# The sum over the experts moved from VectorE to GpSimd, with new instruction orders

## The reference

```python
        out = jnp.zeros_like(x_flat)
        for e in range(N_EXPERTS):
            h = jax.nn.gelu(x_flat @ w1[e] + b1[e], approximate=False)
            y = h @ w2[e] + b2[e]
            out = out + comb[:, e:e + 1] * y
```

## Time and profile before

| | us |
|---|---|
| median of 3 runs (lowest to highest) | 3891.53 (3889.09 to 3901.82) |
| the profiled execution: its own time | 3896.18 |
| its span, first to last instruction | 3893.9 |
| DVE busy | 3420.1 |
| PE busy | 3127.3 |
| ACT busy | 2925.3 |
| POOL busy | 1337.2 |

### The profile page before, as it was taken

How to read it: one execution, slowest core, us unless ns; L and a number is a source line. 1 busy time by engine, 2 the same in 40 slices (tenths; PEclk the granted TensorE clock), 3 DMA queues, 4 the chain that set the end, 5 groups by cost and what they waited for, 6 DMA issues and landing times.

```text
span 3893.9 us, 31221 instructions
## 1 busy us (share of the span) xinstructions
PE 3127.3 (80%) x8728; PEld 1368.3 (35%) x8728; DVE 3420.1 (88%) x4654; ACT 2925.3 (75%) x3806; POOL 1337.2 (34%) x644
## 2 busy tenths in 40 slices
PE   5655878889787788979888888979788887877797
PEld 3231423334343333424343333424343333432232
DVE  1499979999898999999999999999999998999822
ACT  2546887987868888787888878787888879686442
POOL 0254333333323334343433443343433433333200
PEclk8757788989888899989999999989989999888797
DMA  1233333424324243333434342343424333333310
GB/s 63 77 108 96 113 109 92 128 80 135 99 94 118 93 131 95 119 118 109 125 98 123 107 131 94 121 117 109 124 95 126 104 116 104 104 119 104 100 49 11
DMA packets 209022, 404.60 MB, mean 104 GB/s; under 512 B 25936, under 2 KB 34256, under 8 KB 208592
## 3 DMA queue, kind: packets, MB, share of 16 engines
q1 hardware_dynamic: 206800, 398.41, 32.8%
q0 software_dynamic: 2048, 4.20, 1.0%
HBM read 387.57 MB, written 14.94 MB: 103 GB/s over the span
## 4 chain that ended last, share of the span: by engine, by line
PE 37%; DVE 26%; ACT 25%; issue 12%; POOL 0%; DMA 0%; DVEq 0%; ACTq 0%; POOLq 0%
PE bank_a L569 8%; DVE states L921 7%; PE bank_b L580 7%; ACT L705 6%; DVE states L927 6%; ACT decay L705 6%; DVE y_sum L932 3%; ACT L701 3%; ACT tok L705 3%; ACT last L705 3%; ACT middle L705 3%; PE bank_p L478 1%; PE bank_c L397 1%; PE bank_p L421 1%; PE bank_c L640 1%
## 5 line engine op out<-in xcount | busy, mean ns | idle before, releaser
L1199 POOL TENSOR_TENSOR dbu<-dtu,b_rows 128x1024 f32<-128x1024 f32 x512 | 1243.4, 2431 | 2104.1 <-DVE states L921 1823.6
L921 DVE TENSOR_TENSOR_SCAN states<-decay,dbu 128x512 f32<-128x512 f32 x1024 | 1298.7, 1311 | 38.1 <-ACT decay L705 30.5
L705 ACT ACTIVATE decay<-dt,neg_a 128x508 f32<-128x508 f32 x1024 | 659.4, 707 | 64.6 <-DVE states L921 59.0
L705 ACT ACT_TABLE_LOAD x516 | 662.0, 1283 | 47.5 <-PEq L344 16.6
L569 PE MATMUL bank_a<-middle,experts 128*128 128x512 f32 x1024 | 616.2, 687 | 97.1 <-ACT middle L705 88.9
L705 ACT ACTIVATE middle<-bank_a,columns 128x512 f32<-128x512 f32 x608 | 417.8, 687 | 329.6 <-PE bank_a L569 305.4
L927 DVE TENSOR_TENSOR states<-states,c_rows 128x512 f32<-128x512 f32 x960 | 610.8, 679 | 0.3
L932 DVE TENSOR_TENSOR y_sum<-y_sum,states 128x512 f32<-128x512 f32 x960 | 609.9, 674 | 0.2
L580 PE MATMUL bank_b<-middle,experts 128*128 128x512 f32 x1024 | 572.7, 643 | 21.4 <-ACT middle L705 11.8
L705 ACT ACTIVATE last<-bank_c 128x512 f32<-128x512 f32 (+2 forms) x320 | 201.0, 634 | 198.0 <-PE bank_c L617 52.4
L701 ACT ACT_TABLE_LOAD x232 | 297.7, 1283 | 46.0 <-PE bank_p L469 17.0
(11 more groups left out here) (206 smaller groups left out, 3944.7 us busy)
## 6 DMA issues: line engine op xcount, KB each, us to landing
b_rows<-bc_scratch SPq DMA_DIRECT2D x512, 256.0 KB, 3.4
c_rows<-bc_scratch SPq DMA_DIRECT2D x512, 256.0 KB, 3.3
experts<-ew SPq DMA_DIRECT2D x128, 512.0 KB, 3.5
comb_rows<-comb_scratch SPq DMA_DIRECT2D x128, 256.0 KB, 3.8
h_scratch<-tok SPq DMA_DIRECT2D x16, 256.0 KB, 3.3
x_scratch<-xin SPq DMA_DIRECT2D x16, 256.0 KB, 3.8
xr<-x_scratch SPq DMA_DIRECT2D x16, 256.0 KB, 4.9
h<-h_scratch SPq DMA_DIRECT2D x16, 256.0 KB, 5.3
```

Of the source, the lines that this page charges most:

```text
L705: return nc.scalar.activation(out, in_, func, **more)
L921: tick(nc.vector.tensor_tensor_scan(hs[:, h, ::step], da[:, n % DECAYS, h, ::step], dbu[:, n % AHEAD, h, ::step], 0.0, ALU.mult, ALU.add), ...
L1199: tick(nc.gpsimd.tensor_tensor(dbu[:, n % AHEAD], dtu[:, k % 2], row, ALU.mult), "a_dbu")
```

## The change

DVE's e_t writes even experts into x1 and odd ones into part. The add is a `gpsimd.tensor_tensor` on POOL, in a stream C of its own there. e_t of expert e waits for the add of e - 2 (from e = 2), the first norm of the next group, which writes x1, for the add of expert 6, and the router, which writes part, for that of expert 7. All five ORDER strings are replaced: DVE's is 128 letters shorter, POOL's 129 longer, the others have their old length. Matmuls, activations and transfers are the same in number and size, apart from the table loads that follow from ACT's order.

```diff
@@ ORDER
     "POOL": (
-        "APPPPPPAAAAAAAAAAAAAAAAAAAAAAAAAAPAAPAAAAAAAAAAAAAAAAAAAAAAAAAAAAAAAAAAPAAPAAAAAAAAAAAAAAAAAAAAAAAAAA"
...
+        "ACPPPPPPAAAAAAAAAAAAAAAAAAAAAAAAAPAPAAAAAAAAAAAAAAAAAAAAAAAAAAAAAPAACPAACAAAACAAAAACAACAAACAAACAAACAAAA"
+        "AAAAAPACPAAACAAACAAAACCCCAAACAAAAAAAAAAAAAPACPAACAAACAAAACAAACAAACACCAAAAAAAAAAAAAAPACAACPAACAACAAAAA"
...
@@ -1050,7 +1049,11 @@
             def middle(g):
                 q = 3 * g
-                yield from ln("c_", q, A, s_sq, x1)
+                yield
+                if g:
+                    dve.wait_ge(s["e_acc"], NE * g - 1)
+                dve.wait_ge(s["c_rs"], q + 1)
+                tick(tt(x1, A, s_sq, ALU.mult), "c_ln")
                 yield from ln("c_", q + 1, B, s_sq, x1, "mc1")
...
                 yield
+                if g:
+                    dve.wait_ge(s["e_acc"], NE * g)
                 dve.wait_ge(s["e_lg"], g + 1)
...
                     dve.wait_ge(s[f"e_cb{n % 2}"], 16 * (n // 2 + 1))
-                    if n:
-                        dve.wait_ge(s["e_acc"], n)
+                    if e > 1:
+                        dve.wait_ge(s["e_acc"], n - 1)
                     dve.wait_ge(s["e_y"], NF * (n + 1))
-                    tick(stt(part, B, col(f"eb2_{e}"), cb[:, e % 2], ALU.add, ALU.mult), "e_t")
-                    yield
-                    if e == 0 and g >= 2:
-                        dve.wait_ge(s["a_out"], g - 1)
-                    if e == 0:
-                        dve.wait_ge(s["c_h1"], g + 1)
-                    dve.wait_ge(s["e_t"], n + 1)
-                    tick(tt(h2[g % 2], h2[g % 2] if e else h1[:, :], part, ALU.add), "e_acc")
+                    tick(stt((x1, part)[e % 2], B, col(f"eb2_{e}"), cb[:, e % 2], ALU.add, ALU.mult), "e_t")
@@ the gpsimd block
+            def middle(g):
+                for e in range(NE):
+                    n = NE * g + e
+                    yield
+                    if e == 0 and g >= 2:
+                        pool.wait_ge(s["a_out"], g - 1)
+                    if e == 0:
+                        pool.wait_ge(s["c_h1"], g + 1)
+                    else:
+                        pool.wait_ge(s["e_acc"], n)
+                    pool.wait_ge(s["e_t"], n + 1)
+                    tick(nc.gpsimd.tensor_tensor(h2[g % 2], h2[g % 2] if e else h1[:, :], (x1, part)[e % 2], ALU.add), "e_acc")
...
-            drive("POOL", A=each(scan), P=each(gather))
+            drive("POOL", A=each(scan), P=each(gather), C=each(middle))
```

More of the change, by code:

```diff
@@ new lines @@
+        "PCCDPDCCDCCDCCDPCCPCCPPPDCCPPCCDCCPCCPCPCCCPPCCPCCPCCCCCCPDDCCPPPCCCCPCCPPPCCCPCCCPPPCCCPCCPPCDDCPPC"
+        "CCCPCCDDCPDPCDDCDDCDDPDCDPPCDPPCCDPPCCCPDCPCPCCDDPDDCCDPCCPCCDPCCDDPCCDPPDCCPPDCCPPDCCPDDPCCCCDCCPCC"
+        "DCCPPDDPDDCCDCCCCCDCCCDCCDCCDCCDDPCCDCCDCCPPDCCPCCCCPCDCCPPCDPCPDDCCPPPPCCDCCPPDPCPCPDDPDCPCDDDPCDDP"
+        "PCPPDDCCPPCCCDPCCPCPCCDCPDDCCDCCDCCDCCDDPPCCDPCCDDPPCCPPDCCDPCCPPDCCDCCPDPDCCPCCDCCDCCPCCPCCPDDDDDCC"
+        "CCDCDCCCDCCDCCDDPCCDCCDCCDPPCCPCPDPPCDDPDCPDCCPPDPCPCCPPCDDCPCDPCPDCPDDPCDDCPCPPCPPCCCDPPCCPDDCPCCDC"
@@ new lines @@
+        "DDDPDCCCCDCCDDPPCCPCCPDCCDDCCDCCDCCPCCDPPPCCPPDCCDDCCCCPDCCDCPCCCPCCDDDPDDPPPCCDDDCCDDCCDDCCPDCCPPDC"
+        "CPPCCPPDDPCCDDPCPCCPCPPDDPPCPCCPCCPCCPCPDDCDPCPPCPPDDDCDCDPPDDCPCCPDCCPCCDDDPDPCCDCDCCCDDPCCPDCCDDPC"
+        "CDPDPCCPDPPCCDCCPCDCCCDPPDCCDPCCPPCCPDDDDDCCCCCCDCDCCCDCCDCCDPPPCCDDCCPPCCDCCPPDCCPCCCCPCDCCPPCDPPCD"
+        "DCCPPPCPCDPCCDCPCCPDDCDPCDPPDPPCPPDDDCCPCDCPCCPCCCDDPDPCCDCCDCCDCCDCDCCCDDPPCCDPCCDDPPCCPPPDCCDPCCDD"
+        "PDCCPCDCPPDPPCCDCCDDDDCCDCCPCCPPDDDPCCDCCDDPCCDCCDCCDPPPCCCPCCCPPDDPPCCPPCDCCPDCPDPDCPPCCPDDCCPPDCCP"
@@ new lines @@
+        "PCCDDCDPPCPDDPCDDPCDCCCDCCDCCDCCDCDCCCDCCDDPPCCDCCDCCDCCDCCPCCDPDCCPDCCPPCCPPPDCCPDCCPDDPDCCPCCDCPPC"
+        "CCPDDDCCDDCCDCDCCCDDCCDPCCDCCDPPCCPPCCPPDDPCDCCPDCPPCPPDCCPPDPCPCPCCPCPDDCPCDPPCDDCDDCPPDDDCPPCPCDPC"
+        "CPCCDPDDCCCDPDCCCDCCDDPPCCDPCCPDPPCCPPDCCPDCCDPPDCCDCCDCCPCCDCPPCDPDCCDDDDCCDCCPCCPPCCDDCCDCCDCDCDPC"
+        "CDPCCDCCPPDCCPCCCCPCDCCPPCDPPCDPPDPCPCCCPCCPCPDCDPCCCPPPPCDDPPCCDPCPCCDDDPDCCDDDPDCCDCCDCCDCCDCCDCCP"
+        "DDDPCCDPCCDDPPCCDDPCCPPDPCCPDCCPDDPCCPCCDCCDCCPCCPCPCDDDDDCCPCCPPCCDDPDCCDCCDDPCCDCCDCCPPDCCPPPPCCPP"
@@ new lines @@
+        "DPCPDCCPCDPDCPDPCPCCCDPCCPPCDDPPCPPDCDDPCDPDDCDDPCDCCCDCCDCCDCCDCDCCCDCCDDPPPCCDPCCPPDCCPPDCCPPCCDDD"
+        "CCPDCCPCCPCCDDPDPPCCPDDDCCDDDCCPCCPPPPDCCPDCCDCCDCCPDDCCDCCDCCPDPCCPCCCCPCCDPPDPCPDCCPCDPCPDPCPCCCDP"
+        "CCPPCDDPPCPPDCDCDPDDPDCPDDCDCCCCCDCCDCCDCCDCCDCCDCCDDPPCCCCDCCDCCDCDCCCPCCDPDCCDCCPCCPPPDCCPPDCCDCCP"
+        "CCDCCPCCPCCDDDDPDCCPCCPCCPDDCCDCCDDCCPDDCCCPDPCDPPCPPCCDPDCCPDCCDPPPPCDPPCDPCPCPDDDCPCPCCDPCCCDPPCCD"
+        "PPCCDPPCCDPDCCPDDDPCCDDPCCDCDCCCDCCDDPPCCPDCCPPDCCPPDCCDPPCCDPCCPDDCCPCCDDPDPPCCPDDCCDDDDPCCPPDCCDCC"
@@ new lines @@
+        "DCDCCCDDCCDPPCCDCCDPCCCCPCDPCDPPPPPPCPDCDPCPCCPDPCPCCCDPCPPCPPDDDCCDDPPDDDCDPCDCPCPCCCDPDPCCDCCDCCDC"
+        "CDCCDCCDDPPCCDDPCCDDPPCCPPPDCCPDCCDPDPDCCPCCCCDCCDCCPCCPCCPDDDDDCCDDDCCDCCDDPCCDCCDCCPPDCCPPPCCCCPCC"
+        "DPDPPCCPDCDPPCCPPCDDPCPCCPCCPCPCCDDCPDCDDCPPDDDCDCPPDDPPPCCCDPCCPCCDDDDCCCDDDCCCCCCCCDDCCCDCCDCCCCCC"
+        "DCCDDCCDCDCCCCCCCDCCCCDCCDDDDCCDCCCCCCDCCDCDCDDCCDDCCDCDCCDCDDDCDCCDCCCCCDDCDCDCDDCCCCCCCDCCDCCDCDCC"
+        "CDDCCDCCDCCDCCDCCDCCDDCCCCDCCDCCDCDCCCCCDCCCDCDCCDCCDCCDCCCCDCCCCDCDCCCDDDCCCDDCDDDDDDDDDDDDCDCDDCDC"
@@ L73 @@
+        "CDCCDCCDDCDCDDDCDDCDCDCDCCCDCCDCCDCCDCCDCCDCCDCCCCDCCDCCDCCDCCCCCCCCCCCCCCCCCCCCCCCCCCCCCCCCCCCCCCCD"
         "DDDDDDDDDDDDDDDDDDDDDDDDDDDDDDDDDDDD",
@@ new lines @@
+        "PDCPCDPCCPCDCPPDAADACDDACPCPACDPCDPCPDCPDCPAAAADPADPCCCCPPCAAPDPDPCDPDCCCCCCDCDCDCDCPDCDPCCCPAAAACAP"
+        "CDDCPAAPCDCPDAADAAPCCPCDAPDCACPDDPDPCACDPCCPCCPCPADAACDCDCDCDDAAAPCPCDPCDPCPCDPCPDCAAAAPDCDAPACPPCCC"
+        "PCPAADDADAPDPACCCCCDCDCDCDCADPCDPAAAACPDPCADDCPDAADAPCCPACPCDACDAPCDCPADPDCCPCPCPCPCDCAADAADPADPCDCC"
+        "DDAACPCPACPDCDCCDCPCDPCAAAADCDACPCPCCPCPDADDAAAPDAPPCPAPCPDACDDCDCPDCDPCPAAAAPCDDCPAAACPDCADPADPCCPC"
+        "CPCPCDAADAPCPCDAADPCDACDPCCPCPADAADCDPCDCDDACPACPDCDPCDPCDPCCPCDAADAAAPCPACPPCPPAPDDADPDACCCCCCDCAAA"
@@ new lines @@
+        "DAPAAADACAAAAACADADDPDDDADAAADAADAADDDADCAAAADAAAAADAPADAAAACDDAADAAAACAAAAADADAPDPAAAAAAACAAAAAAAAA"
+        "ADDDDCAPAAAAAAACAAAAAAACAPDADADPAPDAAPAAACDAACADACDACADCCCCCDAAAPAAAAAADAPAAAAACAADADDADDDADAACADADA"
+        "ACDDDADAAAAADACAAADAADAAAACDDAAADAAAAAAAACDADAADACAAAAAAAAAACAAADADADDACAAAAAAADADADADAAAACDAAACAACA"
+        "CACCCCCAAAADAADAACDAAAADAAAAACADAAAAACAADADDADDDADAADAACDAADDDADCAAAADAAAAACDAADADDAAAADAACAAAAAADAA"
+        "DAACDAAAAAADAAADAADAADAAADDCDDDDDDDDDDCDDDCCDCCCCCCDDDDDCDDCDCCCCCCDDDDDDDDDDDDDDDDDDDDDDDDDDDD",
@@ L167 @@
+        "AAAAACAAAAACAAAAAAACCCAACADDCAAAAAAAAAAADAAAAAAAAAAAAAACAACAACAAAAAACAAAACAAACAAACAAAAAACCCAAAAAACAA"
+        "AAACADACCCCDCCCCD",
         "",
```

159 lines of the change are left out of this document (60 added, 99 removed).

## The result

The changed kernel takes 3944.74 us (median of 4 runs, 3932.79 to 3949.21) where the kernel before took 3890.31 us beside it (3888.19 to 3901.82): ratio 1.0127, 95% interval 1.0101 to 1.0153. The forecast was 3864, its range ended at 3926; rival D had 3944. One execution of all, of 10096 us in the kernel with the old head, is left out of its ratio. The profiled execution took 3946.3 us with a span of 3944.5, 50.6 more than before.

What follows compares the result with a forecast made beforehand. DVE was taken to bound the 3526 us between head and tail. Terms -81 + 60 - 25 + 6 + 11 + 1 = -28 gave 3868 us profiled, 3864 as run median; range 3812 to 3926 (8 in 10).

Steps and rivals of the forecast that it cites:

- rival D: Slower by order: groups 5 to 12 idle 18 us instead of 6.6, 91 in place of 11; 3944 us, chance 0.10.
- what the adds do to DVE: Scans and POOL's adds exclude each other in SBUF; scans that meet adds lose 60 us in all (bounds 0 and 122).
- -81: DVE's full stretch: removing the adds saves 72 us of queue and 9 us from adds that met POOL.
- +60: DVE's full stretch: time lost waiting for POOL's adds, 60 us by the count of windows.
- in the 3526 us between, DVE is the bound: From DVE's first scan to behind its last: DVE sets the time, busy 211.5 of 218.1 us in group 8.
- the middle groups: Groups 5 to 12: new strings no longer repeat, 8 groups x 1.4 = 11 us more (bounds 0 and 91).
- groups 1, 3 and 14: Fewer ACT table loads there, 71 us less ACT; of DVE's 77 us idle, 25 us go (bounds 0 and 77).
- Head and tail: Head: more ACT work before the first decay, +6 us (bounds 0 and 12); tail: last add before PE's norm, +1.
- the fourth term: The sum's term for groups 5 to 12, whose new strings don't repeat: +11 us.
- They also drain other streams: Argument against taking the idle of groups 13 and 14, with irregular strings, as the measure for groups 5 to 12.

## Why the prediction was wrong

**Right: what the adds do to DVE.** -81 and +60 make -21. DVE's stretch from first to last scan less its idle went from 3334.6 to 3314.1 us (3526.0 less 191.4, 3556.0 less 241.9): -20.5. DVE's busy time is 3394.0 (forecast 3385), table loads 700 (700), POOL's add 1274 ns in the median (1280), as these rows show, the second for the adds of the earlier trace rows. The scans' mean is 1335 ns, where 1355 was forecast: in the changed kernel the scans took 24 us more than before, and the rest of the waiting fell on other operations (under the old orders it was 44 us on scans, and DVE's work is 3314.1 us there too).
```profile
L920 DVE TENSOR_TENSOR_SCAN states<-decay,dbu x1024: 1194/1215/4640, 179.0 to 3734.9; 128x512 f32<-128x512 f32 x171
```
```profile
L1210 POOL TENSOR_TENSOR middle<-middle x112: 1257/1274/3894, 468.9 to 3859.9; 128x512 f32<-128x512 f32 x112
```
The lock is seen on the timelines of DVE and POOL. An undisturbed pair of scans takes 2.33.
```profile
1806.84 3.36 DVE L920 TENSOR_TENSOR_SCAN states<-decay,dbu 128x512 f32<-128x512 f32 x2
...
1956.75 2.93 DVE L920 TENSOR_TENSOR_SCAN states<-decay,dbu 128x512 f32<-128x512 f32 x2
...
1807.09 2.02 POOL L1210 TENSOR_TENSOR middle<-h,middle 128x512 f32<-128x512 f32 x1 [0.68 <-DVE middle L1111]
...
1956.21 1.26 POOL L1210 TENSOR_TENSOR middle<-middle 128x512 f32<-128x512 f32 x1
```
The add at 1956.21 ends 0.72 after the scans want to start, and they lose 0.60: the remainder less 0.12, as the prediction had it. The add at 1807.09 comes while the first scan runs, waits 0.75, and the second scan loses 1.03 (forecast 1.02). The Trainium skill (SBUF — State Buffer, Who interferes with whom) has this as an exclusive lock; the traces agree, with some 50 us of waiting from seven of eight adds.

**Wrong: "in the 3526 us between, DVE is the bound".** This step failed, and with it the rule that a microsecond of DVE's full stretch is one of the time. DVE idle for only 6.6 of 218 us looked like a bound. But 63 us off DVE alone were worth 3 us (0.9991), 50 off ACT alone 2 (0.9996), both 39. With one relieved, the other still sets the pace. So the -21 had no value of their own, and the move under the old orders cost 9 us instead of gaining; with ACT relieved the same move gained 16 (0.9953 against 0.9996).

**Wrong in size: the middle groups.** The prediction knew that the new strings don't repeat, knew both ends (0 and 91), and took 11, from a shift of 1.4 us a group for which it had no row. DVE's idle there rose by 79 (57.2 to 136.4), 17 a group, what groups 13 and 14 had shown and rival D used (18). The lengths rose by 88, as another 9 us of DVE's work fell into these groups. The new orders are what does it: with the old strings and the adds on POOL the same groups took 74 us less. How it does so is only partly seen. Here are groups 5 to 12 as one stretch, with the columns of the earlier trace rows, before, with the move alone, and in the changed kernel; then DVE's wait for the expert's sum in them, before and after.
```profile
1269.80:3020.60 1750.80, 1474.60 (x4320) 646.60 (x4319) 1693.65 (x2311) 1463.70 (x1904) 660.88 (x319) 0.93 0.37 113
```
```profile
1271.70:3036.50 1764.80, 1484.46 (x4318) 648.75 (x4317) 1688.16 (x2247) 1463.02 (x1904) 744.26 (x382) 0.93 0.36 112
```
```profile
1265.50:3104.50 1839.00, 1550.77 (x4404) 697.14 (x4410) 1702.66 (x2253) 1482.75 (x1926) 767.38 (x387) 0.89 0.35 109
```
```profile
DVE middle L1106 <- PE bank_b L580: 8.1, 13, 1.3
```
```profile
DVE middle L1111 <- PE bank_b L579: 47.2, 24, 8.0
```
That wait makes 39 of the 79 us. PE itself is not kept waiting much longer: its idle rose by 12 us (276 to 288), its busy time by 76. It has 84 matmuls more in these groups, 2%, and its clock is lower: 0.50 for 407 us instead of 239. Both the extra work in these groups and the clock are thus candidates for the 88 us, beside the order of the waits.

An example, PE's timeline in group 8: three waits for a gather, and then matmuls of twice the length.
```profile
2034.54 1.02 PE L568 MATMUL bank_a<-middle,experts 128*128 128x512 f32 x2
2035.40 1.02 PE L579 MATMUL bank_b<-middle,experts 128*128 128x512 f32 x2
...
2040.18 0.42 PE L435 MATMUL bank_p<-weights,tok 128*128 128x128 f32 x2 [2.79 <-DMA tok<-emb,row_tile]
2041.38 0.33 PE L435 MATMUL bank_p<-weights,tok 128*128 128x128 f32 x1 [0.79 <-DMA tok<-emb,row_tile]
2043.55 0.48 PE L435 MATMUL bank_p<-weights,tok 128*128 128x128 f32 x1 [1.84 <-DMA tok<-emb,row_tile]
...
2047.24 1.92 PE L568 MATMUL bank_a<-middle,experts 128*128 128x512 f32 x2
```
The pair of L568 takes 1.02 us at 2.4 GHz and 1.92 at 1.2: the granted clock is 1.00 from 2033.7 to 2036.3 us, before the waits, and 0.50 from 2045.4 to 2049.0, behind them. What the displaced steps and the clock each cost was not separated, so the mechanism behind the 88 us stays open: an order of one engine alone can't be mixed with the others' of the other kernel, since each waits for what its partners do next.

**Right in sign, too small: groups 1, 3 and 14.** DVE's idle there fell by 43 us, forecast 25 (77.2 to 34.1). But group 2 gave 35 back (8.1 to 42.9), which no step had: fewer loads in a group don't say that its neighbours stay as they were. Groups 0, 4, 13 and 15 lost another 20 of idle (48.9 to 28.5).

**Head and tail.** +16.1 for +6; above its bound of 12. The run with the old head shows that it doesn't matter: what the start gains is lost again. A head term had no place in the sum. The tail has +4.5 for +1, and is 211.2 us under the old orders (205.0 before). Under those the adds are the cause, as the tail has 205.5 us with seven of eight cut to 4 columns; under the new ones the order is, as such adds leave it at 209.3.

**The sum again**, with the trace's numbers and the idle by groups: DVE's work -20.5; idle -43.1 (groups 1, 3, 14), +34.8 (group 2), +79.2 (5 to 12), -20.4 (the others); head +16.1, tail +4.5: +50.6. The forecast was -28: of the 79 us between them 68 lie in the term for groups 5 to 12. Rival D had 91 for the fourth term and the rest as in the forecast. Its mechanism is the one that came, but that it met the time to the microsecond is luck: its 12 us too many in the middle stand against 14 too few in head and tail. Its chance of 0.10 was too small, since the nearest rows for an irregular group, those of 13 and 14, were its own. "They also drain other streams" was the reason to set them aside, and it had no row. The Trainium skill (GPSIMD Engine Reference, 4.1 Engine selection), which prefers VectorE for elementwise adds, is borne out by 9 us for the move alone, and not where ACT is relieved, as the move gains there.

## What to carry to other kernels

An engine busy 97% of a stretch isn't shown to be its bound: where two engines hand work to each other in fixed orders, take work off each and then off both before a gain is counted for one. When orders written out by hand are remade, price the new order by the idle that the old one shows in its least regular stretches, and don't take a shift of the start for a shift of the end. Test the move of an operation and the remaking of the orders apart: here the one cost 0.24% and the other a full per cent with the adds on POOL, 3% with them on DVE.

## What the runs showed that was not expected

**PE's clock gives freed PE time back.** 464 columns instead of 512 should take some 56 us off PE (48 of 512 columns of the 616.2 us of L569, an estimate). Its busy time fell by 9 (3127.3 to 3118.4), as the granted clock fell from 0.887 to 0.879: L569 went down by 26 us only, and L580, which was not shortened, up from 572.7 to 586.0.

**The middle groups stick to two lengths.** Under the old orders three kernels have several groups of 218.4 to 218.6 us in a row: the kernel before, the adds on POOL with ACT relieved, where DVE idles 5.3 us in such a group, and all three relieved, where it idles 11.0. With the adds some dbus later it was 221.8 or 221.9 six times in a row, and with DVE alone relieved groups of 218.4 and 222 us take turns. With DVE and ACT relieved they don't settle, 215.4 to 219.8. Where the length settles, the clock falls at the same places of each group; here two stretches of the kernel before, 218.5 us apart, with the columns of the earlier trace rows. The clock in both is 0.50, that is 1.2 GHz, and DVE, ACT and POOL do the same in both:
```profile
1959.50:1969.50 10.00, 6.53 (x8) 2.37 (x9) 10.00 (x12) 9.27 (x16) 3.19 (x1) 0.50 0.29 77
2178.00:2188.00 10.00, 6.58 (x8) 2.42 (x9) 10.00 (x12) 9.29 (x15) 3.19 (x1) 0.50 0.25 74
```
So of the 39 us that DVE and ACT give together, only 14 come from groups 5 to 12 and 16 from groups 13 to 15 (by the cut above). What holds the repeating groups at their length stays open; as each of the two lengths has its own repeating pattern of low clock, the clock is a candidate that no run tested.
